# Reordering the first three steps of a gated-recurrence and ternary-FFN kernel on one core

## The chip, the cores and the metric

The kernel runs on one core of a Trainium2 chip. The metric is the device time of one execution in microseconds (us); lower is better. The engines of the core run side by side, each through its own program in order, and meet only at semaphores: TensorE (PE: matmuls; its weight loads are listed as PEld), VectorE (DVE), ScalarE (ACT), GpSimd (POOL), and SyncE (SP), which here only issues DMAs.

## What is computed

The reference gathers rows of an embedding table, adds a gated linear recurrence over the sequence, and adds a two-layer FFN with ternary weights and a low-rank term. Cut to what matters:

```python
h = take(embed_table, ids)                                   # 64 sequences x 256 tokens, 256 wide
n = layernorm(h)
f, i = sigmoid(n @ Wf.T), sigmoid(n @ Wi.T)
c = g(n @ Wh.T)                                              # g(x) = x + 0.5 if x >= 0, else sigmoid(x)
s[t] = f[t] * s[t-1] + i[t] * c[t],  s[-1] = 0.5             # the reference does it in log space
h = h + s
n = layernorm(h)
r = relu(n @ ternary(w_fc).T * scale_fc + gate * (n @ v.T @ fast_b.T @ u.T))
out = h + (r * r) @ ternary(w_proj).T * scale_proj           # hidden width 1024, rank 16
# ternary(w) = clip(round(w / scale), -1, 1), scale = mean(|w|) over a row
```

## The kernel before

The 16384 tokens are cut into 32 chunks of 512 (two sequences each). A step n works on three chunks at once: it computes the gates and the recurrence of chunk n, the first FFN layer of chunk n-1, and the output product of chunk n-2. Steps 0, 1 and 2 (called `start`, `first` and `second` in the code) are written out apart, since the pipeline fills there and the weights are prepared beside it; from step 3 on all steps are alike (`steady`), and a loop runs most of them.

What one step does on TensorE: `gate(0)` to `gate(5)`, eight 128x512 matmuls each (two halves of the state, `e` = 0 and 1, times forget, input and candidate gate); `project`, 64 matmuls of 256 columns; `low_parts` and `low_sums`, the low-rank term; `wide(f)` and `narrow`, the eight banks of the first FFN layer; and a turn of the recurrence's result back to rows (`turn_hidden`, or `turn_upper` in later steps). ScalarE evicts the gate banks (`evict`), normalises rows (`normalise`, 4 instructions), writes the f16 high parts (`x_high`, `part_high`, `low_high`), clips the FFN banks (`clip`) and squares them in pairs (`square_high` into `sq_hi`, `square` into `sq`). VectorE writes the f16 low parts (`x_low`, `part_low`, `low_low`, `square_low`), does candidate, weighting and scan of the recurrence, the residual sums, the layer-norm statistics (`measure`) and the scaling of the output (`scale_output`). GpSimd gathers the table's rows and turns statistics into `rstd` and `shift` (`root`). Suffix 0 of `stats`, `moments`, `rstd`, `normed`, `x_rows`, `x_cols` is the norm ahead of the recurrence, suffix 1 the norm ahead of the FFN. From chunk 2 on (norm 0) and chunk 1 on (norm 1) the normalised rows are turned to columns by two DMA transposes on SP's queue; before that by TensorE (`turn_normed`) with `cols_high` and `cols_low` copying the result out.

There is no scheduler: what stands in a row on an engine is the order of the code in each engine's `step`, and every dependence is a counted semaphore. A count that waits for the n-th eviction therefore depends on the order in which evictions are written. The bank that `gate(4)` and `gate(5)` write is that of gates 0 and 1, and `wide`'s banks are those of gates 2 to 5, so that these wait for `gate_taken`; gates of the next step wait for `relu_ready` of the FFN banks.

Chains that matter below. Norm 0 of chunk 3, in step 2: `measure_next` (DVE) -> `root(0, 3)` (POOL, L420 to L428) -> `normalise(0, 3)` and `x_high(0, 3)` (ACT, L509 and L516) -> `x_low(0, 3)` (DVE, L1025). Low-rank term of chunk 1, in step 2: `low_parts` (PE) -> `part_high(1)` (ACT, L542) -> `part_low` (DVE, L1307) -> `low_sums` (PE, L771) -> `low_high` and `low_low` -> `narrow` (PE, L884) -> `clip` -> next `wide`. On VectorE `x_low(0, 3)` and `scale_output(0)` stand ahead of `part_low`. The preparation of weights: `sum_fc` and the two w_proj sums (ACT, L634, |w_proj| with an accumulator), `halve_scales`, `mark_below`, `make_ternary`, `scale_u`, `split_u`, `set_relu_scale`, `set_proj_scale` (DVE), `turn_low_rank`, `turn_bound`, `spread_proj_scale` (PE).

## Time and profile before

| | us |
|---|---|
| median of 3 runs | 915.22 |
| lowest and highest run | 912.91, 915.28 |
| the profiled execution, its time | 913.92 |
| its span, first to last instruction | 912.1 |
| PE busy | 880.3 (97%) |
| ACT busy | 788.5 (86%) |
| DVE busy | 755.8 (83%) |
| POOL busy | 418.5 (46%) |

All durations below come from the one profiled execution, whose time is 1.8 us over its span and 1.3 us under the median. A timeline row gives start, busy time, engine, line, operation, output<-inputs, shapes and how many instructions are merged, and in brackets how long the engine had been idle before and what ended that. TensorE has two clock levels, 1.2 and 2.4 GHz; the column PEclk of a stretch is the granted clock as a share of 2.4 GHz.

### The profile page before, as it was taken

How to read it: one execution, taken by the hardware profiler on the slowest of the kernel's cores; microseconds unless marked ns; L12 is line 12 of the kernel's file. 1: busy time of each engine (PE TensorE's matmuls, PEld its weight loads, DVE VectorE, ACT ScalarE, POOL GpSimd, SP SyncE). 2: the span in 40 equal slices, each digit the busy share in tenths (PEclk: the TensorE clock that was granted, in tenths of full speed). 3: DMA queues.
4: the chain of work that ended last, by engine and by line, in shares of the span. 5: the costliest groups of instructions: out<-in, count | busy, mean ns of one | idle time of the engine just before them, and what ended most of it. 6: DMA issues, size and time to landing. Idle time of an engine off the chain costs nothing.

```text
span 912.1 us, 18335 instructions
## 1 busy us (share of the span) xinstructions
PE 880.3 (97%) x5505; PEld 482.1 (53%) x5505; DVE 755.8 (83%) x1338; ACT 788.5 (86%) x1195; POOL 418.5 (46%) x457
## 2 busy tenths in 40 slices
PE   4979999999999999999999999999999999999997
PEld 2435554555555455555455555545555545555554
DVE  6988888788888888888888888888888888888766
ACT  5677998888998888998888899888889988899884
POOL 7446544445544445554444554444555444433110
PEclk9999999999999999999999999999999999999999
DMA  4123434432333443333443233344333334423311
GB/s 146 24 53 68 92 73 87 99 78 69 89 82 75 98 98 61 79 85 74 91 98 78 68 88 82 75 97 98 63 81 89 73 85 97 97 51 82 78 47 47
DMA packets 225372, 72.88 MB, mean 80 GB/s; under 512 B 200134, under 2 KB 220176, under 8 KB 225344
## 3 DMA queue, kind: packets, MB, share of 16 engines
q1 hardware_dynamic: 219200, 68.33, 33.8%
q0 software_dynamic: 6144, 4.21, 2.0%
q8 instruction: 14, 0.23, 0.1%
q14 instruction: 14, 0.11, 0.0%
HBM read 27.68 MB, written 24.64 MB: 57 GB/s over the span
## 4 chain that ended last, share of the span: by engine, by line
PE 85%; DVE 4%; ACT 4%; issue 2%; DMA 2%; SPq 1%; POOL 1%; ACTq 0%; POOLq 0%; DVEq 0%
PE bank L848 33%; PE bank L870 22%; PE y_ps L784 22%; PE bank L884 3%; PE turned L824 1%; ACT sq L584 1%; PE turned L761 1%; ACT normed L509 1%; ACT relu L571 1%; SPq L338 1%; DMA x_cols<-x_rows 1%; PE turned L772 1%; PE turned L771 1%; DMA spill<-hid_blocks 1%; DVE hid L1277 0%
## 5 line engine op out<-in xcount | busy, mean ns | idle before, releaser
L870 PE MATMUL bank<-x_cols,fc_t 128*128 128x512 f16 x1024 | 244.1, 381 | 3.6 <-ACT relu L571 3.6
L420 POOL TENSOR_SCALAR var_eps<-moments 128x4 f32<-128x4 f32 x64 | 59.5, 929 | 387.9 <-DVE moments L1020 387.6
L848 PE MATMUL bank<-x_cols,w_hi 128*128 128x512 f16 x768 | 229.8, 381 | 4.9 <-ACT forget L560 2.0
L848 PE MATMUL bank<-x_cols,w_lo 128*128 128x512 f16 x768 | 229.4, 380 | 0.0
L784 PE MATMUL y_ps<-proj_t,sq_hi 128*128 128x256 bf16 x1024 | 225.6, 273 | 3.0 <-DVE sq_lo L1203 3.0
L784 PE MATMUL y_ps<-proj_t,sq_lo 128*128 128x256 bf16 x1024 | 225.6, 273 | 0.0
L571 ACT ACTIVATE relu<-bank,relu_scale 128x512 f32<-128x512 f32 x256 | 159.3, 689 | 39.6 <-PE bank L884 39.0
L410 POOL DMA_INDIRECT rows_raw<-table,idx_now x128 | 148.0, 1156 | 59.9 <-issue 30.8
L870 PEld LDWEIGHTS bank<-x_cols,fc_t 128*128 128x128 bf16 x1024 | 95.0, 98 | 130.8 <-issue 28.3
L1203 DVE TENSOR_TENSOR sq_lo<-sq,sq_hi 128x1024 f16<-128x1024 f32 x128 | 150.6, 1214 | 5.8 <-ACT sq L584 5.7
L509 ACT ACTIVATE normed<-h,shift,rstd 128x256 f32<-128x256 f32 x256 | 132.7, 601 | 5.4 <-POOL shift L428 5.4
L584 ACT ACTIVATE sq<-relu 128x1024 f32<-128x1024 f32 x128 | 136.3, 1066 | 0.0
L578 ACT ACTIVATE sq_hi<-relu 128x1024 f16<-128x1024 f32 x124 | 132.2, 1066 | 0.0
L848 PEld LDWEIGHTS bank<-x_cols,w_lo 128*128 128x128 f16 x768 | 75.4, 98 | 91.3 <-issue 1.3
L848 PEld LDWEIGHTS bank<-x_cols,w_hi 128*128 128x128 f16 x768 | 71.6, 98 | 91.3 <-issue 8.5
L784 PEld LDWEIGHTS y_ps<-proj_t,sq_hi 128*128 128x128 f16 x1024 | 100.2, 98 | 19.7 <-issue 3.7
L1025 DVE TENSOR_TENSOR x_rows<-normed,x_rows 128x1024 f16<-128x1024 f32 x60 | 73.2, 1221 | 44.5 <-ACT x_rows L516 44.5
L784 PEld LDWEIGHTS y_ps<-proj_t,sq_lo 128*128 128x128 f16 x1024 | 100.1, 98 | 14.7
L425 POOL TENSOR_TENSOR rstd<-var_eps,minus_half 128x4 f32<-128x4 f32 x64 | 93.0, 1453 | 5.3
L1016 DVE BATCH_NORM_STATS2 stats<-h 128x6 f32<-128x256 f32 x252 | 88.3, 413 | 3.2
L1277 DVE TENSOR_TENSOR_SCAN hid<-forget,value 128x256 f32<-128x256 f32 x128 | 81.5, 678 | 5.9 <-DVE value L1263 4.6
L516 ACT ACTIVATE x_rows<-normed 128x1024 f16<-128x1024 f32 x60 | 63.4, 1057 | 4.7
(143 smaller groups left out, 919.7 us busy)
## 6 DMA issues: line engine op xcount, KB each, us to landing
out<-out_sb SPq DMA_DIRECT2D x31, 512.0 KB, 3.0
spill<-hid_blocks SPq DMA_DIRECT2D x30, 256.0 KB, 2.1
hid_rows<-spill SPq DMA_DIRECT2D x120, 64.0 KB
rows_raw<-table,idx_now POOLq DMA_INDIRECT x128, 2.6
x_cols<-x_rows SPq DMA_TRANSPOSE x120, 3.6
sq<-w_fc SPq DMA_DIRECT2D x1, 1024.0 KB, 5.5
pj_raw<-w_proj SPq DMA_DIRECT2D x1, 1024.0 KB, 4.8
out<-out_sb SPq DMA_DIRECT2D x2, 256.0 KB, 2.1
```

Of the source, the lines that this page charges most:

```text
L410: pool.indirect_dma_start(rows_raw[:, par, j, :], None, table, bass.IndirectOffsetOnAxis(ap=idx_now[:, par, j:j + 1], axis=0), bounds_chec ...
L425: pool.tensor_tensor(rstd[k][:, :], var_eps[k][:, :], minus_half[:, :], ALU.pow)\
L509: act.activation(normed[k][:, j, :], rows[:, j, :], ACT.Identity, bias=shift[k][:, j:j + 1], scale=rstd[k][:, j:j + 1]).then_inc(normed_re ...
L571: act.activation(relu[:, p, f % 2, :], fc_bank(f, par)[:, :], ACT.Relu, scale=relu_scale[:, f:f + 1]).then_inc(relu_ready, 1)
L578: act.activation(sq_hi[:, 2 * p:2 * p + 2, :], relu[:, p, :, :], ACT.Square).then_inc(sq_hi_ready, 1)
L584: act.activation(sq[:, p, :, :], relu[:, p, :, :], ACT.Square).then_inc(sq_ready, 1)
L784: ins = pe.matmul(y_ps[:, j, :], part[:, f, j * P:(j + 1) * P], proj_t[:, f, :], start=(f == 0 and j % 2 == 0 and part is sq_hi), stop=(f ...
L848: ins = pe.matmul(gate_bank(p, par)[:, :], w[:, k, q, :], x_part(0, par, part)[:, :, k, :], start=(k == 0 and w is w_hi and part == 0), st ...
L870: ins = pe.matmul(fc_bank(f, par)[:, :], fc_t[:, f, k, :], x_part(1, 0, part)[:, :, k, :], start=(opens and k == 0 and part == 0), stop=(n ...
L1016: dve.bn_stats(stats[k][:, j, :], rows[:, j, :]).then_inc(stats_ready[k], 1)
L1203: dve.tensor_tensor(sq_lo[:, 2 * p:2 * p + 2, :], sq[:, p, :, :], sq_hi[:, 2 * p:2 * p + 2, :], ALU.subtract).then_inc(sq_lo_ready, 1)
L1277: dve.tensor_tensor_scan(hid[:, e, at], forget[:, e, at], value[:, e, at], 0.5, ALU.mult, ALU.add).then_inc(scanned, 1)
```

## The change

Nothing is added or dropped; instructions change places in the program's first three steps, and the semaphore counts that depend on the order follow.

- Step 0, ACT: the two w_proj sums go from the end of step 0 to behind the first gate eviction.
- Before step 0, PE: `turn_low_rank` goes from behind `gate(0)` to ahead of it; on DVE `scale_low_rank` goes ahead of `cols_low(0)`, and `split_low_rank` behind the statistics of chunk 1.
- Steps 0 and 1, DVE: the guard, sum and statistics of chunk 2 go ahead of `split_u`; `set_relu_scale` goes behind `cols_low(1)`; the w_proj scales are worked out ahead of the candidate; `residual(1, 1)` goes ahead of w_proj's `make_ternary`.
- Step 1, PE: `turn_hidden(1)` goes from between `wide(6)` and `wide(7)` to behind `spread_proj_scale`.
- Step 1, ACT: `normalise(0, 2)` goes ahead of `low_high(0)`; the squares of chunk 0 are spread: only pair 0 stays in step 1, pairs 1, 2 and 3 stand among the evictions of step 2.
- Step 2, ACT: the gates are evicted in the order forget, input, candidate. `part_high(1)` stands between `normalise(0, 3)` and `x_high(0, 3)`.
- Step 2, DVE: three `square_low`, then `x_low(1, 1)`, then the statistics of chunk 3, then the fourth `square_low`.

ScalarE, the end of step 1 and step 2 up to the normalisation for the FFN. Before (banks 2, 3 and 0, 1 at L571 are FFN banks, at L560 gate banks):

```order
L578 ACTIVATE sq_hi<-relu 128x1024
L584 ACTIVATE sq<-relu 128x1024
L578 ACTIVATE sq_hi<-relu 128x1024
L584 ACTIVATE sq<-relu 128x1024
L560 ACTIVATE cand_sig<-bank2,w_back 128x512
L560 ACTIVATE cand_lin<-bank2,w_back 128x512
L560 ACTIVATE inp<-bank1,w_back 128x512
L560 ACTIVATE forget<-bank0,w_back 128x512
L560 ACTIVATE forget<-bank3,w_back 128x512
L560 ACTIVATE inp<-bank0,w_back 128x512
```

The same place of the changed kernel:

```order
L578 ACTIVATE sq_hi<-relu 128x1024
L560 ACTIVATE forget<-bank0,w_back 128x512
L584 ACTIVATE sq<-relu 128x1024
L560 ACTIVATE inp<-bank1,w_back 128x512
L578 ACTIVATE sq_hi<-relu 128x1024
L584 ACTIVATE sq<-relu 128x1024
L560 ACTIVATE cand_sig<-bank2,w_back 128x512
L560 ACTIVATE cand_lin<-bank2,w_back 128x512
L560 ACTIVATE forget<-bank3,w_back 128x512
L509 ACTIVATE normed1<-h1,shift1,rstd1 128x256 x4
L560 ACTIVATE inp<-bank0,w_back 128x512
L516 ACTIVATE x_rows1<-normed1 128x1024
```

The banks of gates 0 and 1 are now emptied before the squares of pairs 1 and 2 are through, and the fourth pair stands behind all evictions of the step.

VectorE, step 2, from the squares' low parts to `part_low`. Before:

```order
L1203 TENSOR_TENSOR sq_lo<-sq,sq_hi 128x1024 x2
L1016 BN_STATS stats0<-h0 128x6 x4
L1020 BN_AGGR moments0<-stats0 128x2 x4
L1203 TENSOR_TENSOR sq_lo<-sq,sq_hi 128x1024 x2
L1025 TENSOR_TENSOR x_rows1<-normed1,x_rows1 128x1024
L1254 TENSOR_TENSOR cand<-cand_lin,cand_sig 128x512
L1263 TENSOR_TENSOR value<-inp,cand 128x512
L1277 SCALAR_TENSOR_TENSOR hid<-forget,value 128x256 x2
L1284 STREAM_TRANSPOSE hid_blocks<-hid 128x512
L1025 TENSOR_TENSOR x_rows0<-normed0,x_rows0 128x1024
L1211 TENSOR_TENSOR y_sb<-y_ps,proj_scale 128x1024
L1307 TENSOR_TENSOR part_lo<-turned,part_hi 128x512
```

The same place of the changed kernel:

```order
L1216 TENSOR_TENSOR sq_lo<-sq,sq_hi 128x1024 x3
L1038 TENSOR_TENSOR x_rows1<-normed1,x_rows1 128x1024
L1029 BN_STATS stats0<-h0 128x6 x4
L1033 BN_AGGR moments0<-stats0 128x2 x4
L1216 TENSOR_TENSOR sq_lo<-sq,sq_hi 128x1024
L1267 TENSOR_TENSOR cand<-cand_lin,cand_sig 128x512
L1276 TENSOR_TENSOR value<-inp,cand 128x512
L1290 SCALAR_TENSOR_TENSOR hid<-forget,value 128x256 x2
L1297 STREAM_TRANSPOSE hid_blocks<-hid 128x512
L1038 TENSOR_TENSOR x_rows0<-normed0,x_rows0 128x1024
L1224 TENSOR_TENSOR y_sb<-y_ps,proj_scale 128x1024
L1320 TENSOR_TENSOR part_lo<-turned,part_hi 128x512
```

The statistics of chunk 3 (`stats0`, `moments0`) now stand behind `x_low(1, 1)` (`x_rows1`), which waits for ScalarE.

VectorE, the end of step 0. Before:

```order
L1016 BN_STATS stats1<-h1 128x6 x4
L1020 BN_AGGR moments1<-stats1 128x2 x4
L1121 SCALAR_TENSOR_TENSOR u_1<-u_1,u_inv 128x128
L1124 CAST u_hi<-u_1 128x128
L1127 COPY u_parts<-u_hi 128x32x16
```

The same place of the changed kernel:

```order
L1029 BN_STATS stats1<-h1 128x6 x4
L1033 BN_AGGR moments1<-stats1 128x2 x4
L1017 TENSOR_SCALAR rows_fin<-rows_raw 128x1024
L1023 SCALAR_TENSOR_TENSOR h0<-rows_raw,rows_fin 128x1024
L1029 BN_STATS stats0<-h0 128x6 x4
L1033 BN_AGGR moments0<-stats0 128x2 x4
L1134 SCALAR_TENSOR_TENSOR u_1<-u_1,u_inv 128x128
```

Chunk 2's work now follows the statistics of chunk 0 at once, and `x_cols1` (`cols_low(1)`) comes behind `split_u` instead of behind chunk 2.

The diff, cut to its core:

```diff
@@ ACT, step 0
                 if start:
                     evict(0, par, 0, 0, forget, ACT.Sigmoid)
+                    act.wait_ge(pj_in, 16)
+                    for k in range(KD):
+                        act.activation(pj_a[:, k, :], pj_raw[:, k, :], ACT.Abs, accum_out=pj_s[:, 0, k:k + 1])\
+                            .then_inc(abs_summed, 1)
                     evict(0, par, 0, 1, inp, ACT.Sigmoid)
...
                     scale_fc(0)
-                    act.wait_ge(pj_in, 16)
-                    for k in range(KD):
...
@@ ACT, step 1
                     part_high(0)
+                    normalise(0, 2, h0[:, 0, :, :])
                     low_high(0)
-                    normalise(0, 2, h0[:, 0, :, :])
                     x_high(0, 2)
-                    back(1)
+                    for f in range(4):
+                        clip(0, f, par)
+                    square_high(0, 0)
+                    clip(0, 4, par)
+                    clip(0, 5, par)
+                    square(0, 0)
+                    clip(0, 6, par)
+                    clip(0, 7, par)
                     return
@@ ACT, step 2
...
+                    square_high(0, 3)
+                    square(0, 3)
                     normalise(0, 3, h0[:, 1, :, :])
+                    part_high(1)
                     x_high(0, 3)
-                    part_high(1)
                     low_high(1)
@@ PE
             turn_normed(0)
+            turn_low_rank()
...
-                    gate(0)
-                    if start:
-                        turn_low_rank()
-                    gate(1)
-                    gate(2)
+                    for p in range(3):
+                        gate(p)
...
                 wide(6, False)
-                if first:
-                    turn_hidden(1)
                 wide(7, False)
                 if first:
                     spread_proj_scale()
+                    turn_hidden(1)
@@ DVE, ahead of step 0
+            scale_low_rank()
             cols_low(0)
-            scale_low_rank()
             guard(1, 64, 1)
             guard_sum(1, 1)
-            split_low_rank()
             dve.wait_ge(h0_ready, 2)
             measure(0, 1, h0[:, 1, :, :])
+            split_low_rank()
@@ DVE, step 0
-                    split_u()
-                    set_relu_scale()
                     guard(2, 64, 0)
                     guard_sum(2, 0)
+                    dve.wait_ge(h0_ready, 3)
+                    measure(0, 2, h0[:, 0, :, :])
+                    split_u()
                     return
@@ DVE, step 1
-                    measure_next()
                     cols_low(1)
+                    set_relu_scale()
                     part_low()
+                    halve_scales(pj_s, FC + KD, HID)
+                    spread_scales()
...
+                    residual(1, 1)
                     make_ternary(pj_raw, pj_a, pj_s, pj_c, range(KD), pj_ready)
                     set_proj_scale()
-                    residual(1, 1)
-                    guard(3, 64 * 2, 1)
                     guard_sum(3, 1)
```

## Rows read from the trace of the kernel before

**Rows 1.** The page's first part: busy time, share of span, instructions.

```profile
PE 880.3 (97%) x5505; PEld 482.1 (53%) x5505; DVE 755.8 (83%) x1338; ACT 788.5 (86%) x1195; POOL 418.5 (46%) x457
```

**Rows 2.** PE's waits, 20 to 110 us: total, times, longest.

```profile
PE bank L848 <- ACT forget L560: 2.0, 2, 1.3
```

**Rows 3.** PE's timeline in steps 0 to 3.

```profile
24.42 0.58 PE L712 MATMUL y_ps<-ident,a_nb 16*128 16x16 f32 x2
...
30.37 1.91 PE L730 MATMUL turned<-ident,normed 128*128 128x128 f32 x8
...
48.80 1.91 PE L730 MATMUL turned<-ident,normed 128*128 128x128 f32 x8 [0.68 <-ACT normed L509]
53.01 0.62 PE L761 MATMUL turned<-x_cols,low_a 128*32 128x512 f16 x4 [2.29 <-DVE x_cols L1035]
53.56 3.03 PE L870 MATMUL bank<-x_cols,fc_t 128*128 128x512 f16 x8
...
61.33 1.90 PE L870 MATMUL bank<-x_cols,fc_t 128*128 128x512 f16 x8 [2.04 <-ACT relu L571]
...
85.80 0.40 PE L761 MATMUL turned<-x_cols,low_a 128*32 128x512 f16 x4
...
88.59 0.38 PE L771 MATMUL turned<-part_hi,spread 128*128 128x512 f16 x1 [0.56 <-DVE part_lo L1307]
...
97.75 0.60 PE L848 MATMUL bank<-x_cols,w_hi 128*128 128x512 f16 x2 [0.62 <-DMA x_cols<-x_rows]
```

**Rows 4.** Busy time by stretch: length, PE, PEld, DVE, ACT, POOL, PEclk, DMA share, GB/s.

```profile
50.00:53.00 3.00, 0.66 (x4) 0.20 (x2) 2.92 (x10) 2.46 (x5) 0.97 (x3) 0.91 0.29 53
53.00:56.50 3.50, 3.49 (x13) 1.27 (x14) 1.98 (x3) 0.60 (x1) 2.55 (x5) 0.59 0.00 0
```

**Rows 5.** DVE's timeline in steps 0 to 2.

```profile
25.11 0.19 DVE L1056 CAST a_hi<-y_ps 128x32 f16<-128x32 f32 x1 [0.66 <-PE y_ps L712]
...
77.25 0.38 DVE L1020 BATCH_NORM_AGGREGATE moments<-stats 128x2 f32<-128x6 f32 x4
...
85.50 1.22 DVE L1025 TENSOR_TENSOR x_rows<-normed,x_rows 128x1024 f16<-128x1024 f32 x1
...
87.76 0.68 DVE L1307 TENSOR_TENSOR part_lo<-turned,part_hi 128x512 f16<-128x512 f32 x1
```

**Rows 6.** ACT's timeline in steps 0 to 2.

```profile
39.98 1.04 ACT L634 ACTIVATE out_sb<-pj_raw 128x1024 f32<-128x1024 f32 x1
...
60.61 2.41 ACT L571 ACTIVATE relu<-bank,relu_scale 128x512 f32<-128x512 f32 x4
62.89 1.07 ACT L578 ACTIVATE sq_hi<-relu 128x1024 f16<-128x1024 f32 x1
63.84 1.07 ACT L584 ACTIVATE sq<-relu 128x1024 f32<-128x1024 f32 x1
...
79.88 1.06 ACT L516 ACTIVATE x_rows<-normed 128x1024 f16<-128x1024 f32 x1
80.84 0.67 ACT L560 ACTIVATE cand_sig<-bank,w_back 128x512 f32<-128x512 f32 x1
81.41 0.68 ACT L560 ACTIVATE cand_lin<-bank,w_back 128x512 f32<-128x512 f32 x1
82.29 2.08 ACT L509 ACTIVATE normed<-h,shift,rstd 128x256 f32<-128x256 f32 x4 [0.20 <-POOL shift L428]
```

**Rows 7.** POOL's timeline: statistics turned into rstd and shift.

```profile
51.87 0.23 POOL L420 TENSOR_SCALAR var_eps<-moments 128x4 f32<-128x4 f32 x1 [3.75 <-DVE moments L1020]
...
53.61 0.20 POOL L428 TENSOR_TENSOR shift<-minus_mean,rstd 128x4 f32<-128x4 f32 x1
...
72.55 1.18 POOL L422 TENSOR_SCALAR minus_mean<-moments 128x4 f32<-128x4 f32 x1
...
77.72 1.11 POOL L420 TENSOR_SCALAR var_eps<-moments 128x4 f32<-128x4 f32 x1 [1.76 <-DVE moments L1020]
```

**Rows 8.** The page's DMA issues: operation, count, KB each, us to landing.

```profile
pj_raw<-w_proj SPq DMA_DIRECT2D x1, 1024.0 KB, 4.8
```

53 lines of the change are left out of this document (39 added, 14 removed).

## The prediction, on record before the changed kernel ran

> **What bounds the kernel now.** I read the page first: TensorE is busy 880.3 us of a span of 912.1, 97% [rows 1]. From step 3 on it is the bound, so no move of other engines' work there could pay; the change touches only steps 0 to 2, and what it is worth is how much earlier or later TensorE enters step 3. Next the waits of TensorE from 20 to 110 us and its timeline. The idle pieces that the change could reach are few: 2.0 us for the eviction of a forget gate, in two waits (0.7 and 1.3) [rows 2], and in the timeline 0.68 and 2.29 us on both sides of the turn of chunk 0's normalised rows, 2.04 us for the first clipped bank, 0.56 us for `part_low` in step 2 and 0.62 us for the columns of chunk 3 [rows 3]. Third, the table by stretch: around that turn the granted clock falls. In 53.0 to 56.5 it averages 0.59, that is mostly the 1.2 GHz level, and before that TensorE had worked 1.91 us of the 4.9 from the end of the gates (48.1) to 53.0 [rows 3, 4]. The eight matmuls at 53.56 take 3.03 us there and 1.90 at 61.33 [rows 3]: the fall costs 1.1 us. All of it together is about 9 us, so the whole purse of this change is 1% of the time.
>
> From here "at X" is a time in the trace of before, and "moves by" is how much earlier (minus) or later (plus) the same work comes after the change. I follow TensorE from place to place.
>
> **Place 1, the low-rank turn and chunk 1's statistics.** TensorE's three small matmuls between gates 0 and 1 (end at 25.0 [rows 3]) now fill the idle time before gate 0. VectorE's wait for them, 0.66 us [rows 5], goes, and the three small instructions behind it (0.19 the first [rows 5], some 0.4 in all) stand behind the statistics. So statistics, GpSimd's root and ScalarE's normalisation of chunk 1 move by -1.0, and with them the eight transposes at 30.37, which run at the pace of that normalisation [rows 3]. ScalarE must have its new work done by then: two w_proj sums of 1.04 us [rows 6] from the end of the first eviction (24.9) to 27.1, then an eviction of 0.67, done at 27.7; the normalisation starts at 28.7. The sums wait for w_proj, which lands 4.8 us after its issue [rows 8]; the issue is at 17.3, so it is there at 22.1. Cost nothing, with 1.0 us of cover; if w_proj came 3 us later, this gain were gone. Place 1: -1.0.
>
> **Place 2, step 1's gates.** The w_proj sums no longer stand ahead of step 1's evictions at 39.98 to 42.06 [rows 6], which removes the shorter of the two waits for `forget`, 0.7 us [rows 2]. TensorE ends the gates 1.7 us earlier, at 46.4. But it then waits for chunk 0's normalisation, and that hardly moves. VectorE hands its statistics over 1.0 us earlier. GpSimd's root then meets VectorE's guard and sum of chunk 2, which now follow at once. A root takes 1.94 us when VectorE leaves it alone (51.87 to 53.81), and one of its instructions that takes 0.23 alone takes 1.18 beside such a 1024-wide sum [rows 7]. I take 0.8 us more for this root, so the turn at 48.80 moves by -0.2 only. Bounds: 0 and 1.9 us more.
>
> **Place 3, low_parts at 53.01.** Its 2.29 us wait was for VectorE's `cols_low(1)` behind chunk 2's sum and statistics. Now `cols_low(1)` stands behind `split_u` and is limited by ScalarE's copy, which ends some 0.2 earlier than before, at 51.1; then 0.6 us for the second half: TensorE goes on at 51.7. Moves by -1.3. The stretch before it is as thinly filled as before (1.9 us of 5.3), so I expect the same fall of the clock and the same 1.1 us, and count no gain. Bounds: -1.1 if it doesn't fall, 0 if it does.
>
> **Place 4, the wait for the first clip at 61.33.** Before, `x_high(0, 2)` and the normalisation of chunk 2 (2.1 us) stood between `low_high(0)` and the first clip at 60.61 [rows 6]. The normalisation is now done while TensorE computes, between `part_high(0)` and `low_high(0)` (52.8 to 54.9; `low_high` can start at 55.8). The first clip starts when the narrow matmuls deliver, at 57.9: -2.7, and so does the `wide` at 61.33.
>
> **Place 5, step 2's gates and project.** Turning the recurrence of chunk 1 behind `wide(7)` costs nothing: its scan ends at 62.6 by my count (VectorE, from 57.0: guard 0.7, scan 1.2, `x_low` 1.2, candidate and weighting 1.4, scan 1.3), and TensorE gets there at 63.3. The gates move by -2.7 (to 64.2), and the 1.3 us wait for `forget` inside them [rows 2] goes, as banks 0 and 1 are emptied first. Project starts 4.0 us earlier; w_proj's turned columns land at about 73.3, ahead of 74.7. `low_parts` at 85.80 moves to 81.8 [rows 3].
>
> **Place 6, where the gain is lost: low_sums at 88.59.** TensorE ends its two open `wide` at 84.0 and then needs `part_low`. On VectorE that stands behind `x_low(0, 3)` and `scale_output`, and behind the whole chain of chunk 3's norm 0, which starts with statistics that the change puts behind `x_low(1, 1)`. So I need the end of `x_high(1, 1)` on ScalarE. From the first clip at 57.9 its queue is full: 8 clips of 0.57 (four from 60.61 to 62.89), 6 squares of 0.95 (62.89 to 63.84), 6 evictions of 0.57 (80.84 to 81.41), one normalisation of 2.1 and the `x_high` of 1.06 [rows 6], 4.6 + 5.7 + 3.4 + 2.1 + 1.1 = 16.9, and 0.9 of waiting for gates 0 and 1, whose evictions stand ahead of squares: 75.7. Before, it ended at 80.94 [rows 6], so this piece does gain 5.2. But then VectorE: `x_low(1, 1)` 1.2, statistics 1.8, done at 78.7; before they were done at 77.6 [rows 5]. They come **1.1 us later** than before. Root: before 77.72 to 82.29, 4.6 us, beside two-input instructions of VectorE [rows 6, 7]. Now it meets one 1.2 us `sq_lo`, candidate and weighting, and I take 3.7; bounds 1.9 (alone [rows 7]) and 4.6. Normalisation at 82.4, against 82.29: +0.1. `part_high(1)` now stands between it and `x_high(0, 3)`: +0.5. From `x_low(0, 3)` at 85.50 to `part_low`'s end at 88.44 [rows 5] nothing changes. So `low_sums` moves by **+0.6** (bounds -1.2 and +1.5): 5.2 us of idle TensorE stand at 84.0 to 89.2 where there were 0.56.
>
> Here a rule of the Trainium skill bears. The page "SBUF — State Buffer", section "SBUF: two separate sides", says that VectorE instructions with two SBUF inputs and GpSimd instructions that read SBUF exclude each other for a whole instruction. The rows of GpSimd agree (1.18 against 0.23), but they show no root beside a scan; by the rule a scan would hold it too. That is a rival below.
>
> **Place 7, the clock after that idle time.** 5.2 us without work is thinner than the stretch before 53.0, so the clock should fall again. If it lasts as long as in [rows 4], it can cost from 0 (spent in the idle time) to 1.7; the row's price is 1.1. I take 0.9. (The skill's page "TensorE: Matmul & The Clock Gate", under its heading on HAM oscillation, likewise holds that idle gaps bring the clock down and the ramp has to be paid again; the fall at 53 agrees.)
>
> **Place 8, the columns of chunk 3.** The recurrence of step 2 reaches the spill earlier, and the transposes queued on SP behind it too, so that the 0.62 us wait at 97.75 [rows 3] goes: -0.6. Behind that TensorE bounds again and carries the difference to the end.
>
> **Sum.** +0.6 + 0.9 - 0.6 = +0.9 us. Against the profiled execution's own 913.92 that is 914.8, and against the median, 915.22, it is 916.1; the three runs lie 2.4 us apart, as much as two falls of the clock. I take the middle, **915.5**. 0.3% of the time is 2.7 us, about what a measurement of this kernel can tell from no change: the forecast is no change.
>
> **Rivals.**
> - *The late wait is mild (faster).* Root runs undisturbed (-1.8), the clock falls in neither place (-1.1, -0.9): 915.5 - 3.8 = 911.7. For it: ScalarE may deliver the last square late and leave VectorE idle beside the root. Against: the thin stretches are both still there. 0.15.
> - *The clock stays down (slower).* If after the idle 5.2 us the 1.2 GHz level lasts two times the 3.5 us of [rows 4], it covers 3.4 us of TensorE's full-speed work at double time, some 3.1 after slack, instead of 0.9, with root at 4.6 us (+0.9): 915.5 + 2.2 + 0.9 = 918.6. It decides if the clock is still low when step 3's gates run, at about 97. For it: after `low_sums` TensorE waits again for the clip. Against: the fall at 53 was over by 56.5 although a 2.04 us wait followed. 0.12.
> - *The scan holds the root* (the rule above): up to 1.2 us more: 916.7. 0.10.
> - *No late fall, the rest as forecast*: 914.6. 0.13.
> - *w_proj lands late, or an early move is worth nothing*: the chain of place 6 then starts up to 1 us later, 916.5. 0.05.
>
> **How the numbers follow.** The forecast has 0.45. Faster by over 0.3%: 0.15; within: 0.45 + 0.10 + 0.13 + 0.05 = 0.73; slower: 0.12. The range takes in the bounds of root and clock on both sides, -3.8 and +2.9: 911.7 to 918.4.
>
> **What would show it.** In the profile after: transposes at about 29.4; no wait for `forget`; the first clip near 57.9; project near 74.7; one PE wait of about 5 us at `turned` L771 (its new line) for `part_lo`, ending near 89.2; norm-0 statistics of chunk 3 done near 78.7 and normalised rows near 82.4; PEclk under 1 behind 84. Wrong would be place 6 if that wait is under 3 us or ends before 88, and place 7 if no stretch from 84 to 96 shows a clock under 1.

## The result, and the profile of the changed kernel

The changed kernel takes 919.74 us (median of 5 runs, 918.69 to 920.77); the kernel before, run beside it, 915.21 (912.91 to 915.28). The ratio is 1.0056 with a 95% interval of 1.0041 to 1.007: **4.5 us slower**, outside the forecast range of 911.7 to 918.4, and on the side that had 0.12. The profiled execution took 920.77 us with a span of 918.9; before it was 913.92 and 912.1. So the two traces lie 6.8 us apart, 2.3 more than the medians: each is one execution, and the one of before is below its median, the other above.

The page's first part, which answers [rows 1]: TensorE is busy 4.1 us more with as many instructions, which is for the most part time at the lower clock, and the rest of the 6.8 us of span is idle time.

```profile
PE 884.4 (96%) x5505; PEld 483.7 (53%) x5505; DVE 757.9 (82%) x1338; ACT 788.9 (86%) x1195; POOL 420.3 (46%) x457
```

TensorE's waits from 20 to 130 us, in the columns of [rows 2] (line waited at, tile, releaser: total, times, longest):

```profile
PE turned L788 <- DVE part_lo L1320: 3.5, 1, 3.5
PE y_ps L801 <- DVE sq_lo L1216: 3.0, 1, 3.0
PE turned L746 <- ACT normed L509: 2.6, 2, 2.3
PE bank L865 <- DVE x_cols L1048: 1.8, 2, 1.1
PE bank L887 <- ACT relu L571: 1.5, 2, 0.8
PE turned L778 <- DVE x_cols L1048: 1.4, 1, 1.4
```

Both waits for `forget` of [rows 2] are gone, as meant, and the ones for the clips (`relu`) are down from 2.8 to 1.5 in all. Two long ones are new, both in step 2 and both for VectorE: 3.0 us inside project, for the low part of a square, and 3.5 us for `part_lo`. TensorE's timeline at the places of [rows 3]:

```profile
29.27 1.91 PE L746 MATMUL turned<-ident,normed 128*128 128x128 f32 x8 [0.39 <-ACT normed L509]
...
35.72 0.60 PE L865 MATMUL bank<-x_cols,w_hi 128*128 128x512 f16 x2 [1.08 <-DVE x_cols L1048]
...
49.62 2.17 PE L746 MATMUL turned<-ident,normed 128*128 128x128 f32 x8 [2.25 <-ACT normed L509]
53.20 0.62 PE L778 MATMUL turned<-x_cols,low_a 128*32 128x512 f16 x4 [1.41 <-DVE x_cols L1048]
53.75 3.60 PE L887 MATMUL bank<-x_cols,fc_t 128*128 128x512 f16 x8
...
61.04 1.90 PE L887 MATMUL bank<-x_cols,fc_t 128*128 128x512 f16 x8 [0.77 <-ACT relu L571]
...
85.19 0.37 PE L801 MATMUL y_ps<-proj_t,sq_hi 128*128 128x256 bf16 x1 [2.95 <-DVE sq_lo L1216]
...
88.58 0.40 PE L778 MATMUL turned<-x_cols,low_a 128*32 128x512 f16 x4
88.91 1.90 PE L887 MATMUL bank<-x_cols,fc_t 128*128 128x512 f16 x8
94.36 0.38 PE L788 MATMUL turned<-part_hi,spread 128*128 128x512 f16 x1 [3.55 <-DVE part_lo L1320]
...
94.78 3.18 PE L887 MATMUL bank<-x_cols,fc_t 128*128 128x512 f16 x8
```

Place by place: the first turn comes 1.1 us earlier, the second 0.8 later, `low_parts` at 53.20 against 53.01, the `wide` behind the first clip 0.3 us earlier, `low_parts` of step 2 2.8 later (88.58), `low_sums` 5.8 later (94.36 against 88.59). One step on, in step 3, it is 6.4 later (121.96 against 115.54), and at the end 6.8.

The table by stretch, as in [rows 4] (length, PE, PEld, DVE, ACT, POOL, granted clock, DMA share, GB/s):

```profile
53.20:57.70 4.50, 4.50 (x14) 1.58 (x15) 3.76 (x15) 2.94 (x6) 3.21 (x3) 0.50 0.36 73
...
85.00:88.40 3.40, 3.21 (x16) 2.25 (x16) 3.30 (x6) 0.69 (x2) 3.16 (x5) 0.50 0.00 0
91.00:94.30 3.30, 0.00 (x0) 0.00 (x0) 2.96 (x3) 0.22 (x1) 2.67 (x3) 1.00 0.35 63
95.20:98.60 3.40, 3.40 (x15) 0.88 (x13) 2.92 (x5) 0.38 (x1) 0.00 (x0) 0.50 0.66 123
```

Between 26 us and the program's last 2 us the clock is at 1.2 GHz in three stretches, where the trace of the kernel before has one: around the second turn (the eight matmuls at 53.75 take 3.60 us against 3.03 in [rows 3]), at the end of project, and behind the idle time of 91.0 to 94.3, where eight matmuls take 3.18 us (1.90 at full speed [rows 3]).

VectorE's timeline in the changed kernel, to lay beside [rows 5]:

```profile
30.89 1.77 DVE L1119 TENSOR_SCALAR u_pow<-u_max 128x8 int32<-128x8 int32 x1
...
72.43 1.22 DVE L1023 SCALAR_TENSOR_TENSOR h<-rows_raw,rows_fin 128x1024 f32<-128x1024 f32 x1
73.56 3.49 DVE L1216 TENSOR_TENSOR sq_lo<-sq,sq_hi 128x1024 f16<-128x1024 f32 x3
80.78 1.23 DVE L1038 TENSOR_TENSOR x_rows<-normed,x_rows 128x1024 f16<-128x1024 f32 x1 [3.72 <-ACT x_rows L516]
...
83.35 0.38 DVE L1033 BATCH_NORM_AGGREGATE moments<-stats 128x2 f32<-128x6 f32 x4
...
93.53 0.68 DVE L1320 TENSOR_TENSOR part_lo<-turned,part_hi 128x512 f16<-128x512 f32 x1
```

ScalarE in steps 1 and 2, beside [rows 6]:

```profile
60.30 2.43 ACT L571 ACTIVATE relu<-bank,relu_scale 128x512 f32<-128x512 f32 x4 [0.72 <-PE bank L901]
...
73.75 0.69 ACT L560 ACTIVATE forget<-bank,w_back 128x512 f32<-128x512 f32 x1
77.15 2.08 ACT L509 ACTIVATE normed<-h,shift,rstd 128x256 f32<-128x256 f32 x4 [2.71 <-POOL shift L428]
...
79.70 1.05 ACT L516 ACTIVATE x_rows<-normed 128x1024 f16<-128x1024 f32 x1
...
87.71 2.08 ACT L509 ACTIVATE normed<-h,shift,rstd 128x256 f32<-128x256 f32 x4 [3.92 <-POOL shift L428]
```

GpSimd, beside [rows 7]:

```profile
30.65 1.01 POOL L410 DMA_INDIRECT rows_raw<-table,idx_now  x1 [0.30 <-issue]
31.66 0.97 POOL L397 MEMSET rows_raw<- 128x1024 f32 x1
...
72.29 1.05 POOL L425 TENSOR_TENSOR rstd<-var_eps,minus_half 128x4 f32<-128x4 f32 x1
73.42 3.70 POOL L428 TENSOR_TENSOR shift<-minus_mean,rstd 128x4 f32<-128x4 f32 x1
83.82 1.32 POOL L420 TENSOR_SCALAR var_eps<-moments 128x4 f32<-128x4 f32 x1 [6.71 <-DVE moments L1033]
```

The instruction at 73.42 is the `shift` of chunk 1's norm 1. In the kernel before it stood here:

```profile
75.76 0.21 POOL L428 TENSOR_TENSOR shift<-minus_mean,rstd 128x4 f32<-128x4 f32 x1
```

Read backwards from TensorE's wait at 94.36, these rows are one chain. `part_lo` ends at 94.2, behind `x_low(0, 3)` and `scale_output`, behind ScalarE's normalisation of chunk 3 (87.71), behind GpSimd's root (83.82), behind the statistics of chunk 3 (83.7), behind `x_low(1, 1)` (80.78), which waited 3.72 us for `x_high(1, 1)` (ends 80.75), behind `normalise(1, 1)` (77.15), which waited 2.71 us for **one GpSimd instruction: `shift`, 128x4, 0.21 us long before, took 3.70 us here** while VectorE ran a `guard_sum` and three `sq_lo` back to back. A second small instruction is swollen the other way: VectorE's `u_pow` took 1.77 us at 30.89, just while GpSimd issued a gather (1.01 us) and cleared a buffer (0.97 us).

### The profile page after: what moved, and what is told of

Its sections match the earlier page's. It is cut to its first block, busy times and chain, and to the rows that moved or that the text cites. A ratio compares the mean times of both kernels' runs of the same rounds, so it can differ in the third digit from the quotient of the medians.

```text
span 918.9 us, 18335 instructions
## 1 busy us (share of the span) xinstructions
PE 884.4 (96%) x5505; PEld 483.7 (53%) x5505; DVE 757.9 (82%) x1338; ACT 788.9 (86%) x1195; POOL 420.3 (46%) x457
## 4 chain that ended last, share of the span: by engine, by line
PE 82%; DVE 5%; ACT 4%; issue 3%; DMA 2%; POOL 2%; SPq 1%; ACTq 0%; DVEq 0%; POOLq 0%
PE bank L865 31%; PE bank L887 22%; PE y_ps L801 21%; PE bank L901 4%; PE turned L841 1%; ACT sq L584 1%; PE turned L778 1%; ACT relu L571 1%; ACT normed L509 1%; SPq L338 1%; DMA rows_raw<-table,idx_now 1%; PE turned L788 1%; DMA x_cols<-x_rows 1%; PE turned L789 1%; DVE stats L1029 1%
## 5 line engine op out<-in xcount | busy, mean ns | idle before, releaser
L571 ACT ACTIVATE relu<-bank,relu_scale 128x512 f32<-128x512 f32 x256 | 159.3, 690 | 41.9 <-PE bank L901 41.3
L865 PEld LDWEIGHTS bank<-x_cols,w_hi 128*128 128x128 f16 x768 | 71.7, 98 | 89.2 <-issue 7.5
```

The lines of the kernel that those rows point to most:

```text
L571: act.activation(relu[:, p, f % 2, :], fc_bank(f, par)[:, :], ACT.Relu, scale=relu_scale[:, f:f + 1]).then_inc(relu_ready, 1)
L865: ins = pe.matmul(gate_bank(p, par)[:, :], w[:, k, q, :], x_part(0, par, part)[:, :, k, :], start=(k == 0 and w is w_hi and part == 0), st ...
```

## The experiments

Every kernel below computes the whole of the reference; the three with idle matmuls (8, 11 and 12) add work and take none away. The theory of this section: the loss is made in step 2, where the order of VectorE puts chunk 3's statistics behind `x_low(1, 1)`, and a shut-out GpSimd makes it larger. The rivals: the shut-out alone; the early moves of steps 0 and 1; the clock.

All in one table first. Times in us in the profiled execution; low_sums is TensorE's start at `turned<-part_hi`; the ratio is against the kernel before on the same chip, whose medians were 915.21 for the first kernel, 912.92 for the runs 1 to 4, 913.84 for 5 to 8 and 912.56 for 9 to 12.

| kernel | first clip | project | low_sums, step 2 | low_sums, step 3 | span | median | ratio [95%] |
|---|---|---|---|---|---|---|---|
| before | 60.61 | 78.72 | 88.59 | 115.54 | 912.1 | 915.21 | 1 |
| changed | 60.30 | 76.83 | 94.36 | 121.96 | 918.9 | 919.74 | 1.0056 [1.0041, 1.007] |
| 1 changed, again | 59.76 | 76.29 | 93.78 | 121.39 | 917.0 | 918.74 | 1.0059 [1.0042, 1.0076] |
| 2 statistics first | 60.58 | 77.12 | 89.60 | 117.19 | 912.9 | 912.27 | 0.9998 [0.9988, 1.0008] |
| 3 VectorE waits for shift | 59.22 | 75.75 | 90.43 | 117.87 | 914.1 | 916.46 | 1.0042 [1.0025, 1.0059] |
| 4 step 2 as before | 60.17 | 78.30 | 88.16 | 115.02 | 910.4 | 912.20 | 0.9994 [0.9984, 1.0004] |
| 5 only step 2 changed | 60.80 | 77.44 | 93.41 | 121.92 | 918.1 | 918.77 | 1.0053 [1.0036, 1.007] |
| 6 gather behind u | 58.20 | 74.73 | 92.26 | 119.92 | 916.2 | 918.17 | 1.005 [1.0034, 1.0067] |
| 7 part_low first | 60.11 | 76.64 | 86.12 | 116.91 | 913.2 | 913.94 | 1.0 [0.9991, 1.001] |
| 8 clock held | 57.98 | 74.54 | 92.10 | 120.60 | 917.3 | 918.79 | 1.0055 [1.0038, 1.0071] |
| 9 statistics, then x_low | 59.22 | 75.75 | 92.37 | 119.67 | 915.3 | 916.44 | 1.0041 [1.0026, 1.0057] |
| 10 columns first | 60.22 | 76.75 | 86.25 | 115.86 | 911.2 | 912.01 | 0.9995 [0.9986, 1.0004] |
| 11 all together | 56.40 | 72.96 | 82.45 | 110.91 | 906.5 | 908.40 | 0.9957 [0.9944, 0.9971] |
| 12 before, clock held | 58.61 | 77.68 | 87.51 | 114.33 | 909.9 | 911.22 | 0.9986 [0.9977, 0.9995] |

The span less the last low_sums column is 795.3 to 796.9 us in all fourteen: from step 3's `low_sums` on they are one kernel to within 1.6 us, and the difference is made ahead of it.

How far can a single trace be trusted ahead of that point? Eight of these kernels (the changed one and runs 1, 2, 3, 4, 7, 9 and 10) differ in nothing that the first clip waits for. Yet it comes between 59.22 and 60.58. It goes with the fall of the clock in step 1, which lasts 6.8 us in all eight but begins anywhere from 49.1 us (run 3, clip at 59.22) to 52.0 (run 2, clip at 60.58). The trace of the kernel before is late by itself, too: TensorE's first gate starts at 20.66 there, and in runs 5 and 12, which have the same steps ahead of it, at 20.13 and 19.99. So a difference of up to 1.4 us between two traces can be chance, and where an edit lies in step 2, what it moved is best counted from the first clip on. The medians, of four executions or more, suffer less from it.

**1. The changed kernel again**, unchanged, beside runs 2 to 4, on one chip.

> The changed kernel, unchanged. It asks whether what its one profile shows repeats: shift of norm 1 on GpSimd (chunk 1) taking 3.7 us, ScalarE waiting 2.7 us for it, low_sums of step 2 at 94.4, two falls of the clock in step 1 and one after the long wait. If these are the cause, all repeat within 1 us and the time is 918.5 to 921. A second thing is open: one small VectorE instruction in step 0 (u_pow) took 1.8 us. If that is a rule of this order it is there again; if it is chance it takes 0.2 and steps 0 and 1 run 1.5 us earlier.

The delay is there again, and so are its parts: `shift` 3.70 us, `u_pow` 1.76, the clock down for 6.8, 3.4 and 3.4 us. None of these is chance; the places lie 0.5 to 0.6 us earlier than in the first trace. Runs 2 to 4 are compared with this one (918.74 us).

**2. Statistics of chunk 3 ahead of the squares**, in step 2 on VectorE:

```diff
                 if second:
+                    measure_next()
                     square_low(0, 0)
                     square_low(0, 1)
                     square_low(0, 2)
                     x_low(1, 1)
-                    measure_next()
```

> The changed kernel with the statistics of chunk 3 ahead of all four square_low and of x_low in step 2. They take 1.8 us in which GpSimd isn't shut out (no statistics row did that), and they no longer wait for ScalarE. My theory (place 6: the statistics behind x_low make part_low late): statistics done near 75.5, chunk 3 normalised as soon as ScalarE has emptied its queue at about 81, part_low no longer the last to come; low_sums at 85 to 87 rather than 94.4 and a time of 911 to 913, under the kernel before. Rival (the loss is in steps 0 and 1, the long wait in step 2 would be there anyway for another reason, such as ScalarE's queue): low_sums stays over 90 and the time over 916.

The loss is gone: 6.5 us less than the changed kernel. The profiled execution took 914.68 us, 2.4 over the median. In it `low_sums` moved by 4.2 us (5.0 counted from the first clip), less than expected: with the statistics done at 75.8 the wait for `part_lo` is still 2.9 us, because `x_low(0, 3)` and `scale_output` still stand ahead of it. VectorE and GpSimd in this kernel's timeline:

```profile
75.40 0.38 DVE L1033 BATCH_NORM_AGGREGATE moments<-stats 128x2 f32<-128x6 f32 x4
...
73.70 0.29 POOL L428 TENSOR_TENSOR shift<-minus_mean,rstd 128x4 f32<-128x4 f32 x1
```

`shift` begins here at the same point of VectorE's work, in the last fifth of a `guard_sum`; behind that comes a statistics instruction instead of a two-input one, and it takes 0.29 us. So this edit removes both suspects at once, and runs 3 and 9 are there to part them.

**3. VectorE waits for shift** and nothing else changes its place:

```diff
                 if second:
+                    dve.wait_ge(rstd_ready[1], 2)
                     square_low(0, 0)
```

> The changed kernel with one wait more: in step 2 VectorE's first square_low also waits until GpSimd has set shift for chunk 1's norm 1. Theory (GpSimd is shut out as long as VectorE runs two-input instructions back to back): shift ends near 74 rather than 77.1, ScalarE normalises at about 74.5, x_low of norm 1 starts near 78.2 rather than 80.8, and low_sums comes at about 91.8 rather than 94.4; the time is 2.5 us under the changed kernel, although VectorE waits more. Rival (GpSimd's instruction was slow for a reason of its own, or another wait takes over): shift still takes 3 us or low_sums stays within 1 us of 94.4, and the time stays at 919.5 to 920.

The row of GpSimd and the one of TensorE's waits:

```profile
72.33 0.29 POOL L428 TENSOR_TENSOR shift<-minus_mean,rstd 128x4 f32<-128x4 f32 x1
...
PE turned L788 <- DVE part_lo L1320: 5.1, 1, 5.1
```

`normalise(1, 1)` starts at 73.24 instead of 76.60, the wait in project (3.0 us) is gone, `low_sums` comes 3.35 us earlier (2.8 counted from the first clip) and the time falls by 2.3 us, or 1.6 by the ratios; the slowest of these four runs (917.54) is under the fastest of run 1 (917.63). So the shut-out of `shift` costs some 2 us, between a third and a half of the loss. The rest stays: statistics at 79.82, 5.1 us of wait.

**4. Step 2 and the squares as before**, only the moves of steps 0 and 1. Against the changed kernel, on ScalarE and VectorE:

```diff
-                    for f in range(4):
-                        clip(0, f, par)
-                    square_high(0, 0)
...
+                    back(1)
                     return
                 if second:
-                    square_high(0, 1)
...
+                    evict_low()
...
-                if second:
-                    square_low(0, 0)
-                    square_low(0, 1)
-                    square_low(0, 2)
-                    x_low(1, 1)
-                    measure_next()
...
```

> The changed kernel with step 2, and the squares of chunk 0, as in the kernel before: only the moves in steps 0 and 1 are left. Theory (step 2's order is what costs): steps 0 and 1 give 0 to 3 us, so 912 to 915.5. Rival (the moves in steps 0 and 1 cost, by the longer fall of the clock at 51 to 58 and the slower root): 916 or more.

No difference that can be measured. The early half of the change neither costs nor brings much. In its trace the clock is down for 6.8 us in step 1 instead of 3.4; that isn't the early half's doing, as run 5, which has the old steps 0 and 1, shows 6.8 too. And `shift` took 2.56 us, but that was hidden, since the normalisation after it started at 77.36, no later than in the kernel before (77.78).

**5. The complement**: the kernel before with step 2's part of the change alone (squares spread, evictions in the new order, VectorE's new order). Against the kernel before it is the diff of run 4 with its signs turned round:

```diff
-                    back(1)
+                    for f in range(4):
+                        clip(0, f, par)
+                    square_high(0, 0)
...
+                if second:
+                    square_low(0, 0)
+                    square_low(0, 1)
+                    square_low(0, 2)
+                    x_low(1, 1)
+                    measure_next()
...
```

> The kernel before with only the step 2 part of the change (squares of chunk 0 spread, forget evicted first, statistics of chunk 3 behind x_low, part_high between normalise and x_high), steps 0 and 1 as before. Theory (step 2's order costs, and the moves of steps 0 and 1 give little): the long wait for part_low is there, low_sums of step 2 at 92 to 95, and the time 4 to 7 us over the kernel before, 917 to 920. Rival (the loss needs both halves together): within 2 us of the kernel before.

The whole loss: +4.9 us, where both halves together made +4.5 and, in run 1, +5.8. TensorE's waits:

```profile
PE turned L787 <- DVE part_lo L1323: 5.1, 1, 5.1
...
PE y_ps L800 <- DVE sq_lo L1219: 1.4, 1, 1.4
```

In this kernel `shift` took 0.21 us, yet the statistics come at 82.78, since the root began 2.2 us later than in the changed kernel (its own statistics are as late as in the kernel before) and the evictions and `x_high(1, 1)` still stand ahead. The new order of step 2 is the cause of the loss: the statistics wait for whatever makes `x_high(1, 1)` late, and the shut-out of `shift` is one such thing, not the only one.

**6. GpSimd's gather waits until u is scaled**, in step 0:

```diff
             root(0, 1)
+            pool.wait_ge(u_scaled, 1)
             gather(2, 0, (2, 3))
```

> The changed kernel with one wait more, on GpSimd: its last two gathers for chunk 2 and the clearing behind them start only when VectorE has set u_inv. Theory (the two lock each other out in both directions: VectorE's u_pow, 0.2 us of work, stood 2.0 us until GpSimd's clearing had ended): u_pow takes 0.2 us again, the candidate of step 0 starts at about 31.9 rather than 33.1, and the wait of 1.1 us in step 1's gates for the columns of chunk 1 goes; by then 1 us is won, of which the slower root takes most again; the time is 0.5 to 1 us under the changed kernel. Rival (u_pow is slow for its own reason): it still takes 2 us and nothing moves.

VectorE's and GpSimd's rows:

```profile
30.90 0.17 DVE L1120 TENSOR_SCALAR u_pow<-u_max 128x8 int32<-128x8 int32 x1
...
32.44 1.19 POOL L410 DMA_INDIRECT rows_raw<-table,idx_now  x1 [3.83 <-DVE u_inv L1126]
```

`u_pow` is back at 0.17, and the early places come within 0.3 us of the forecast: the first clip at 58.20 (forecast 57.9), project at 74.73 (forecast 74.7). A part of that is luck: `low_parts` of step 1 is 1.1 us earlier than in run 1 (51.82 against 52.91), the clip 1.6, and the 0.5 between them is the clock, which was down for 3.4 us here and for 6.8 in run 1. But `low_sums` gains 1.5 us only, and the ratio, 1.005 against 1.0059 in run 1, 0.8 us, within the intervals: GpSimd is still shut out in step 2 (3.70 us), and the clock, down for 6.8 us from 82.1, takes up TensorE's work there.

**7. part_low first**: run 2, and `part_low` ahead of `x_low(0, 3)` and `scale_output` on VectorE, `x_high(0, 3)` ahead of `part_high(1)` on ScalarE.

```diff
-                    x_low(0, 3)
-                    scale_output(0)
                     part_low()
+                    x_low(0, 3)
+                    scale_output(0)
                     low_low()
```

> The kernel with chunk 3's statistics first in step 2 (its time was 912.3, low_sums at 89.6 after a wait of 2.9 us), and two swaps more: x_high(0, 3) ahead of part_high(1) on ScalarE, and part_low ahead of x_low(0, 3) and scale_output on VectorE. Theory (what was left of the wait was part_low's place behind these): TensorE waits under 0.7 us at low_sums, which comes at about 87, the clock doesn't fall behind it, and the time is 2.5 to 3.5 us under that kernel, 909 to 910. Rival (part_low isn't what holds TensorE, or low_low is late instead): under 1 us gained.

`low_sums` is at 86.12 with no wait at all, 2.5 us ahead of the kernel before, and the time doesn't follow. TensorE's row in step 3, and SyncE's:

```profile
97.43 0.60 PE L865 MATMUL bank<-x_cols,w_hi 128*128 128x512 f16 x2 [2.01 <-DMA x_cols<-x_rows]
...
87.73 4.52 SPq L338 DMA_DIRECT2D hid_rows<-spill  x4
92.36 3.17 SPq L305 DMA_TRANSPOSE x_cols<-x_rows  x2
```

Chunk 3's transposes stand behind four fetches on SyncE that wait for the spill, so they start at 92.4 as before (92.68), however early the rows are ready. TensorE waits 2.0 us for them where it waited 0.62 [rows 3], and the clock goes down behind that, at 98.6 for 3.4 us. The gain of step 2 is given back in step 3.

**8. The clock held over the thin stretch** of step 1: the changed kernel with idle matmuls (128x512, into a bank that is overwritten later) on both sides of the second turn.

```diff
                     if first:
+                        hold(8)
                         turn_normed(1)
+                        hold(5)
```

> The changed kernel with idle work for TensorE in step 1: 8 matmuls of 512 columns ahead of the turn of chunk 0's normalised rows, where it waits 2.2 us, and 5 behind it, where it waits 1.4 us, into a bank that nothing else uses yet. It asks what the fall of the clock at 50 to 58 costs. Theory: with TensorE busy there the granted clock stays at 2.4 GHz, the 8 wide at 53.8 take 1.9 rather than 3.6 us, and low_sums of step 1 comes 1.7 us earlier; behind that ScalarE is the bound, so that low_sums of step 2 moves by 1 us at most and the time by 0.5 to 1.5 us. Rival (the clock falls although it is busy, or the filling delays the transposes): nothing gained.

Two stretches of this kernel, in the columns of [rows 4]:

```profile
50.00:57.00 7.00, 6.50 (x34) 2.84 (x33) 5.84 (x20) 6.88 (x14) 5.45 (x7) 1.00 0.43 83
...
92.10:98.00 5.90, 5.40 (x18) 1.42 (x18) 4.15 (x6) 1.07 (x2) 0.30 (x1) 0.51 0.65 120
```

The fall of the clock in step 1 is gone and the first clip comes 1.8 us earlier (57.98 against 59.76), `low_sums` 1.7. But behind the same long wait the clock now stays down for 6.8 us instead of 3.4, and the time is the same within the intervals (1.0055 against 1.0059). So the clock in step 1 isn't what made the loss, and an earlier front was no gain here while the wait for `part_lo` stood.

**9. Statistics behind the squares, ahead of x_low**, so that `shift` stays shut out but the statistics don't wait for ScalarE:

```diff
                     square_low(0, 2)
-                    x_low(1, 1)
                     measure_next()
+                    x_low(1, 1)
```

> The changed kernel with one swap on VectorE in step 2: the statistics of chunk 3 ahead of x_low(1, 1) instead of behind it, still behind three square_low. Theory (the order of statistics and x_low is worth most of the loss, apart from the 3.7 us in which GpSimd is shut out): GpSimd's shift for chunk 1 still takes 3.7 us, since three square_low still follow each other; the statistics end near 78.8 rather than 83.2, chunk 3 is normalised when ScalarE is through with its queue at 83 rather than at 87, low_sums of step 2 comes at 89.5 to 90.5 rather than 93.8, and the time is 3 to 4 us under the changed kernel. Rival (root is the bound whatever the order): normalised at 86 or later, under 1.5 us gained.

`shift` is at 3.70 again and the statistics are done at 77.70, root at 79.72. The gain is smaller than expected: `low_sums` at 92.37, 1.4 us ahead of run 1 (0.9 counted from the first clip), not 3 to 4. TensorE's waits:

```profile
PE y_ps L801 <- DVE sq_lo L1216: 2.9, 1, 2.9
PE turned L788 <- DVE part_lo L1320: 2.9, 1, 2.9
```

I had priced the statistics alone. With `shift` late, everything on ScalarE from `normalise(1, 1)` to the fourth pair of squares is late by 2.7 us too, project waits for the low part of that pair, `low_parts` starts at 87.24, and `part_high(1)` waits for that. In the changed kernel there are thus two chains of nearly the same length to `part_lo`: one over chunk 3's statistics, one over `shift`, ScalarE and project. Run 3 shortens the one over `shift`, run 9 the one over the statistics, and each brings some 2 us (ratios of 1.0042 and 1.0041 against 1.0059, by 1.6 us; by the medians, each less that of the kernel before on its chip, 2.3 and 1.9); run 2 shortens both and brings 5.6 to 6.5.

**10. Chunk 3's columns first**: run 7, and on SyncE in step 2 the transposes of chunk 3 right behind the spill, ahead of the four fetches (with a wait until the gates that read the old columns are through).

```diff
+                if isinstance(n, int) and n == 2:
+                    spill_blocks(n)
+                    sp.wait_ge(gate_done, 6 * n)
+                    turn_rows(0, n + 1, 1 - par)
+                    fetch_rows(n, par)
+                    store(n - 2, par)
+                    return
```

> The kernel in which part_low is never late (low_sums of step 2 at 86.1, time 913.9), with SP's queue in step 2 reordered: the two transposes of chunk 3's columns ahead of the four fetches of the spilled recurrence. There the gain of low_sums was given back in a wait of 2.0 us for these columns at 97.4, and in a fall of the clock behind it. Theory (SP's queue is the last bound of the filling pipeline): the wait goes, no fall at 98, low_sums of step 3 at about 113.3 rather than 116.9, and the time 2.5 to 3.5 us under the kernel before. Rival (the fetched rows come too late for the norm of chunk 2 and TensorE waits for low_parts of step 3 instead): step 3 longer by as much as was won.

The wait for the columns and the fall of the clock in step 3 are gone, and `low_sums` of step 3 is 1.05 us earlier than in run 7. The time is 0.5 us under the kernel before, which the interval can't tell from nothing, and not the 2.5 to 3.5 that I expected. The next bound is in project of step 3:

```profile
102.51 0.27 PE L808 MATMUL y_ps<-proj_t,sq_hi 128*128 128x256 bf16 x1 [1.79 <-DVE sq_lo L1223]
```

**11. All together**: run 10, with run 6's wait on GpSimd and run 8's idle matmuls.

```diff
             root(0, 1)
+            pool.wait_ge(u_scaled, 1)
             gather(2, 0, (2, 3))
...
+                        hold(8)
                         turn_normed(1)
+                        hold(5)
```

> All of it: the reordered SP queue, part_low and the statistics first, GpSimd's gathers held back until u_inv is set, and TensorE kept busy by 8 and 5 idle matmuls in step 1. Theory (each gain is carried once nothing behind it is the bound): the first clip at 57 rather than 60, project at 73.5, and all places behind move with it by 2 to 3 us; time 5 to 6.5 us under the kernel before, 907.5 to 909. Rival (ScalarE's full queue or a wait for DMAs in step 2 takes over): under 3.5 us.

908.40 us, 4.2 under the kernel before and, by the ratios, some 9 under the changed one: **it beats both**. Two stretches of it, first the one around the second turn, then the start of step 3:

```profile
51.00:54.00 3.00, 2.68 (x15) 1.20 (x16) 2.79 (x15) 2.93 (x7) 1.83 (x4) 1.00 0.67 128
...
90.00:96.00 6.00, 6.00 (x29) 2.73 (x28) 3.64 (x11) 6.00 (x8) 0.47 (x1) 1.00 0.36 105
```

From 25 us on no row of this trace shows TensorE's clock down until the program's last 2 us, and no wait of TensorE between 20 and 130 us is longer than 0.9. The three parts are worth little apart: run 10 is 0.5 us under the kernel before, runs 6 and 8 are within the intervals of the changed kernel.

**12. The kernel before with idle matmuls** around the second turn.

```diff
                     if first:
+                        hold(2)
                         turn_normed(1)
+                        hold(9)
```

> The kernel before with idle matmuls alone, 2 ahead of the turn of chunk 0's normalised rows and 9 behind it. It prices the one fall of the clock in the kernel before by itself. Theory: the clock stays at 2.4 GHz at 53, the 8 wide take 1.9 rather than 3.0 us; what follows waits for ScalarE, whose low_high comes 1.1 us earlier, so 0.5 to 1.1 us under the kernel before. Rival (the first clip is bound by ScalarE's normalisation, not by TensorE): under 0.3 us.

TensorE's rows that answer 53.01 and 53.56 of [rows 3]:

```profile
52.36 0.40 PE L761 MATMUL turned<-x_cols,low_a 128*32 128x512 f16 x4 [0.34 <-DVE x_cols L1041]
52.70 1.90 PE L870 MATMUL bank<-x_cols,fc_t 128*128 128x512 f16 x8
```

1.3 us faster than the kernel before, and its interval, 0.5 to 2.1 us, excludes nothing gained. The price of the fall that the prediction took, 1.1 us, is in the second row: 1.90 us for eight matmuls that took 3.03. The 1.3 us is not that price by itself, since the clock falls elsewhere now: at 60.2 for 3.4 us, behind the wait of 2.04 us for the clip, where eight matmuls take 2.84 us.

## Why the prediction was wrong

The mechanism of its place 6 was the right one, and named as the place where the gain is lost: chunk 3's statistics behind `x_low(1, 1)`, a late `part_lo`, a long idle time of TensorE, and the clock behind it. Its size was wrong, +5.8 us for `low_sums` instead of +0.6, and the whole came to +4.5 us by the medians where its sum had +0.9. The steps:

- **Place 1** (turn moves by -1.0): 30.37 to 29.27, right in direction and in part by luck. Some 0.5 us of the 1.1 lies ahead of the change, in the late start of the one trace of before: the turn ends at 32.28 in that trace, at 31.47 and 31.61 in the other two with the old steps (runs 5 and 12), and at 30.6 to 31.2 in those with the new ones. What failed is its silent sequel, that the rest of VectorE's step 0 comes earlier too. With the root, GpSimd's gather came 1.0 us earlier (31.68 to 30.65), `u_pow` behind the statistics only 0.5 (31.44 to 30.89). So it fell on top of that gather and a clear and took 1.77 us, and the candidate of step 0 starts at 33.10 where it started at 32.97 before. Run 6 shows what this cost: 1.1 us at `low_parts` of step 1, 1.6 at the clip and at project.
- **Place 2** (`forget` wait goes, turn -0.2): the wait went; the turn moved by +0.8. Run 6, with `u_pow` at its old length, has it at 48.49, -0.3. The root's +0.8 us was right: from 2.5 us (45.62 to 48.11) to 3.25 (45.69 to 48.94).
- **Place 3** (-1.3): +0.2. In run 6 -1.2. The fall of the clock came as forecast but lasted 6.8 us instead of 3.4, and eight matmuls took 3.60 us instead of 3.03: 0.6 us that no term held. Run 5, with the old steps 0 and 1, has 6.8 us as well, so the length isn't shown to come from the change.
- **Places 4 and 5** (clip 57.9, project 74.7): 60.30 and 76.83, thus -0.3 and -1.9 where -2.7 and -4.0 stood. Both are the sequel of places 1 and 3; in run 6 they are met (58.20 and 74.73).
- **Place 6, the step that failed**: "from the first clip at 57.9 its queue is full", with 0.9 us of waiting, so `x_high(1, 1)` ends at 75.7. It ended at 80.75. Of the 5.0 us, 2.4 came from the late first clip (60.30 for 57.9; `forget` of half 1 ends at 74.4, by the sum's terms it should have at 72.0) and 2.7 from a wait that the sum didn't have, ScalarE's for `shift`. GpSimd's root(1, 1) stands in no term: it was taken as done in time, without a reason. The sum also lacked TensorE's wait of 2.95 us in project for the low part of a square, which goes with `shift` (in run 3 it is gone). With the late start of project and the lower clock at its end, this is why TensorE came to `low_sums` later too, and waited 3.55 us there and not 5.2. What came after was sized well: statistics 3.0 us behind `x_high` (forecast 3.0), root 3.9 (3.7), `low_sums` 6.7 behind the normalisation's start (6.8). The delay went through unchanged: 83.73 for 78.7, 87.71 for 82.4, 94.36 for 89.2. Taking what runs 3 and 6 gave back at `low_sums` (3.35, or 2.8 from the clip on, and 1.5) from run 1's 93.78 leaves 88.9 to 89.5, beside the 89.2 that was forecast; that is a sum, not a run.
- **Place 7** (late fall, +0.9): it came, at 95.2, and eight matmuls took 1.3 us more. Another at 85.0 wasn't foreseen; it lies over the end of project, ahead of the wait for `part_lo`, and is hidden by it.
- **Place 8** (-0.6): the 0.62 us wait for the columns is gone. With place 7: from `low_sums` of step 2 to that of step 3 it is 27.60 us against 26.95, +0.65, where the forecast had +0.3. So place 7 was nearer 1.3 than 0.9, within its bounds. No run takes this fall away by itself.

Of the rivals, "the clock stays down" came nearest in number (918.6, a time that the range, up to 918.4, left out) but with another content: that fall lasted 3.4 us, not two times 3.5, and the late root it assumed was the wrong root. "The scan holds the root" was worth 0.5 us at most and not 1.2: from 86.4 to 87.7 two scans ran beside the root of chunk 3, whose `rstd` took 1.45 us (1.04 alone) and `shift` 0.33 (0.20), and a part of that lies beside the product ahead of the scans. The rule of the Trainium skill behind it ("SBUF — State Buffer", section "SBUF: two separate sides"), that VectorE instructions with two SBUF inputs and GpSimd instructions that read SBUF exclude each other, was the one that decided this case, but at other instructions than the one where I weighed it. It also says that whichever starts first has the pair; `u_pow` behind GpSimd's gather went in that direction, though with its one input it isn't covered by the rule as told here. What it doesn't say, and the rows show, is that a waiting GpSimd instruction can lose at the borders of several VectorE instructions in a row. The Trainium skill's page "Perfetto Trace Analysis", section "GPSIMD Engine Instruction", holds that a GpSimd span in a profile is unreliable by itself; here ScalarE starts `normalise` at 77.15, 0.03 us after the end of the `shift` row, so this span is real.

Most of the trouble with the range has one source: every term of place 6 had a bound, except that the chain's own input, ScalarE's queue, was taken as complete. A second list of "who else could be late for this" (GpSimd for the normalisation) would have led to root(1, 1), of which [rows 7] show an instruction at 72.55, 1.18 us long instead of 0.23: already shut out, and hidden only because ScalarE came to its normalisation late.

## What to carry to other kernels

Before an instruction is put ahead of another in a queue, ask of each what its own inputs wait for: work that feeds a long chain over three engines (statistics, root, normalisation) must not stand behind one that waits for a busy engine. Don't put a run of two-input VectorE instructions where a small GpSimd instruction lies on such a chain; one wait, or one statistics instruction in between, let it through here. In the fill of this pipeline a removed wait was given to the next bound (SyncE's queue, then the low parts of the squares, then the clock), so such edits are to be judged together, and at a point behind which nothing differs any more. And before places of two single traces are laid side by side, look at a place ahead of the edit: what already differs there isn't the edit's.
